# Gated cross-attention with routed experts: next rows quantised earlier, routing moved forward, two more summing steps on GpSimd in three groups of four

## The reference

```
x = x + tanh(g_xattn) * attention(layernorm(x), context)
x = x + tanh(g_ffn)   * ffn(layernorm(x))

attention: q = qdq(x) @ qdq(wq).T + bq;  k, v = split(context @ wkv.T + bkv)
           16 heads of 32;  o = softmax(q k / sqrt(32)) v;  out = qdq(o) @ qdq(wp).T + bp
           qdq rounds each row to 8-bit integers by its largest absolute value
ffn:       32 experts in 4 groups, 4 chosen per token through the best 2 groups by sigmoid(x @ gate_w.T) + bias
           each expert takes its first 128 tokens:  silu(x w1) * (x w3) @ w2, weighted, summed
           plus a shared part:  silu(x @ shared_gate) * (x @ shared_up) @ shared_down
```

## Time and profile before

| what | us |
|---|---|
| median of three runs | 3088.6 |
| lowest and highest run | 3077.08, 3096.61 |
| the profiled execution, its time | 3097.04 |
| its span in the trace | 3095.3 |

### The profile page before, as it was taken

How to read it: one execution, slowest core, us unless ns; L and a number is a source line. 1 busy time by engine, 2 the same in 40 slices (tenths; PEclk the granted TensorE clock), 3 DMA queues, 4 the chain that set the end, 5 groups by cost and what they waited for, 6 DMA issues and landing times.

```text
span 3095.3 us, 42827 instructions
## 1 busy us (share of the span) xinstructions
PE 2759.0 (89%) x14612; PEld 1140.5 (37%) x14652; DVE 1918.4 (62%) x3814; ACT 1369.7 (44%) x2436; POOL 1809.2 (58%) x1558
## 2 busy tenths in 40 slices
PE   5898999899989988989899899989999889997987
PEld 3333333333333333333333333333332334443766
DVE  6577667766776677667767766776676334343222
ACT  4155545654564466455545654564455410110111
POOL 0186667666666685667576757665677432424455
PEclk9799999999999999999999999999999999999999
DMA  3111012101211031103111311220112123232995
GB/s 127 36 51 52 24 35 73 54 22 35 76 52 40 18 91 47 44 13 98 37 35 25 97 27 36 62 65 22 35 49 63 69 89 123 72 112 70 299 292 114
DMA packets 146584, 215.56 MB, mean 70 GB/s; under 512 B 24984, under 2 KB 78232, under 8 KB 146368
## 3 DMA queue, kind: packets, MB, share of 16 engines
q1 hardware_dynamic: 130496, 195.95, 20.9%
q0 software_dynamic: 15872, 16.87, 3.0%
HBM read 126.49 MB, written 34.24 MB: 52 GB/s over the span
## 4 chain that ended last, share of the span: by engine, by line
PE 64%; DVE 14%; ACT 7%; DMA 6%; issue 6%; SPq 2%; POOL 1%; another core or an unknown queue 1%; POOLq 0%; ACTq 0%; DVEq 0%
PE o_ps L873 11%; PE s_ps L859 10%; PE r_all L748 9%; PE r_all L777 8%; PE r_all L787 8%; DVE piece_max L1312 7%; PE r_all L828 6%; DMA out_rows<-probs,slot_init 4%; ACT probs L1096 4%; PE sum_ps L886 3%; PE r_all L846 3%; SPq L555 1%; DVE amax L1166 1%; PE sum_ps L894 1%; POOL prob_acc L1581 1%
## 5 line engine op out<-in xcount | busy, mean ns | idle before, releaser
L1581 POOL TENSOR_TENSOR prob_acc<-prob_acc,probs 128x512 f32<-128x512 f32 x1140 | 1431.9, 1291 | 380.8 <-ACT probs L1096 379.2
L1096 ACT ACTIVATE probs<-s_ps 128x512 f32<-128x512 f32 (+1 forms) x1664 | 936.9, 596 | 762.6 <-PE s_ps L859 736.2
L1312 DVE TENSOR_REDUCE piece_max<-r_all 128x1 f32<-128x400 f32 (+1 forms) x2048 | 1024.9, 565 | 128.2 <-PE r_all L787 123.6
L787 PE MATMUL r_all<-k_flat,q_stack 96*128 96x400 f16 (+1 forms) x2048 | 608.5, 351 | 100.2 <-DVE piece_max L1312 55.1
L859 PE MATMUL s_ps<-q_stack,k_flat 97*128 97x512 f16 (+1 forms) x1664 | 625.8, 395 | 57.4 <-ACT probs L1096 50.6
L873 PE MATMUL o_ps<-probs,v_sb 128*32 128x512 f32 (+1 forms) x3328 | 462.5, 629 | 21.4 <-ACT probs L1096 21.4
L859 PEld LDWEIGHTS s_ps<-q_stack,k_flat 97*128 97x128 f16 (+1 forms) x1664 | 158.1, 100 | 616.0 <-ACT probs L1096 430.0
L1578 POOL COPY prob_acc<-probs 128x512 f32<-128x512 f32 x128 | 73.1, 615 | 501.9 <-PE sum_ps L894 367.1
L787 PEld LDWEIGHTS r_all<-k_flat,q_stack 96*128 96x128 f16 x2048 | 203.1, 100 | 394.5 <-DVE piece_max L1312 202.8
L1613 POOL DMA_INDIRECT slot_rows<-payload,slot x128 | 125.3, 979 | 281.9 <-DVE slot L1490 215.8
L828 PE MATMUL r_all<-probs,k_flat 128*128 128x512 f32 x512 | 223.4, 594 | 2.0 <-DVE sum_sb L1452 1.2
(11 more groups left out here) (220 smaller groups left out, 2714.4 us busy)
## 6 DMA issues: line engine op xcount, KB each, us to landing
k_flat<-k_hi SPq DMA_DIRECT2D x256, 100.1 KB, 2.2
ctx_raw<-in_ctx SPq DMA_DIRECT2D x96, 256.0 KB, 2.9
xin<-in_x SPq DMA_DIRECT2D x16, 1024.0 KB, 5.6
k_flat<-k_lo SPq DMA_DIRECT2D x128, 100.1 KB, 2.2
v_sb<-in_L_ffn_w SPq DMA_DIRECT2D x18, 512.0 KB
q_stack<-q_hi SPq DMA_DIRECT2D x256, 32.0 KB, 1.8
h_rows<-work SPq DMA_DIRECT2D x8, 1024.0 KB, 4.5
x_rows<-xin SPq DMA_DIRECT2D x8, 1024.0 KB, 6.9
```

The source lines that it names most:

```text
L787: last = nc.tensor.matmul(ps[:, 0:w], q_stack[0:KSPLIT, g % 2, j, qt * P:(qt + 1) * P], k_stack[0:KSPLIT, g % 2, j, at:at + w], start=True ...
L1096: nc.scalar.activation(probs[0:w, slot, j, :], s_ps[j % SBANKS][0:w, :], ACT.Exp).then_inc(probs_ready, 1)
L1312: V.reduce_max(piece_max[:, j * TT + qt, i:i + 1], ps[:, 0:PIECE[i]], X_AXIS).then_inc(free_of(*key), 1)
L1581: last = G.tensor_tensor(prob_acc[:, j, :], prob_acc[:, j, :], probs[:, slot, j, :], ALU.add)
```

## The change

- GpSimd adds twelve steps (0 to 11) in the groups 0, 2 and 3 of each batch, TensorE sums only step 12 there. Group 1, and the very last group, stay as they were. That is 46 steps of four adds more on GpSimd and 46 sums fewer on TensorE.
- The parts of the next rows start at step 7 of group 1 (statistics) and go on one a step: square root 8, reciprocal and shift 9, normalising 10 and 11, largest value 12; then in group 2 rounding 0 and 1, clipping 1 and 2, integers 3 and 4.
- `rows_out` writes x1 first, as soon as the statistics for the second norm are made, and `h` after it.
- For the last batch, the transposes `hT` and the logits move into the gate tiles of the batch before, into a buffer of their own; its routing runs between that batch's `add_shared`; its counts come after its first pair of gate tiles, its expert weights and slots after its first `swiglu`. The counts of the batch before come after its own third pair and those logits.
- The slot table is read back on GpSimd's queue.
- Twelve homes: two more sets of expert weights are loaded when the last `up` tile is made, into the places of the shared gate and up weights and of `ctx_lo`, one when the last `down` tile is made, and these stand on SP ahead of the output of the last batch; two more after `out_written`, in the places of the values, as before.

```diff
-PE_SUMS, LAST_PE_SUMS = (4, 8, KT - 1), (2, 4, 6, 8, 10, KT - 1)
+PE_SUMS, LONG_PE_SUMS, LAST_PE_SUMS = (4, 8, KT - 1), (KT - 1,), (2, 4, 6, 8, 10, KT - 1)
...
-FIRST_X, NEXT_X = 1, 1
+FIRST_X, NEXT_X = 1, 6
...
-HOMES, EARLY_HOMES, FREE_HOMES = 9, 7, 5
+HOMES, EARLY_HOMES, FREE_HOMES, GATE_HOMES, DOWN_HOMES = 12, 7, 5, 2, 1
...
-    return PE_SUMS if n + 1 < B * GROUPS else LAST_PE_SUMS
+    if n + 1 == B * GROUPS:
+        return LAST_PE_SUMS
+    return PE_SUMS if n % GROUPS == 1 else LONG_PE_SUMS
...
+def next_x(g, kt):
+
+    return (g - 1) * KT + kt - NEXT_X
...
-    order = gates[0:6] + [("cum", f), ("total", f)] + gates[6:]
+    counts = [("cum", f), ("total", f)]
+    down = [("down", f, t) for t in range(TT)]
+    if f == B - 1:
+        return gates[0:2] + counts + gates[2:] + down
+    if f == B - 2:
+        return (gates[0:2] + [("hT", f + 1, c) for c in range(DC)] + gates[2:3] + [("logitsT", f + 1)] + gates[3:6]
+                + [("logits", f + 1)] + counts + gates[6:] + down)
+    order = gates[0:6] + counts + gates[6:]
...
+def logits_after(f):
+
+    if f == B - 2:
+        return {("logitsT", f + 1): [0], ("up", f, 1): [1], ("gate", f, 2): [2, 3]}
+    return {("logitsT", f + 1): [0], ("down", f, 1): [1], ("down", f, 2): [2, 3]} if f + 1 < B else {}
...
-        hT, actT = probs[:, 0], probs[:, 1]
+        last_hT = ctx_lo_flat[:, 0:2 * DC * N].bitcast(FP32).rearrange("p (c n) -> p c n", c=DC)
+        hT, actT = [probs[:, 0]] * (B - 1) + [last_hT], probs[:, 1]
...
-        homes = free_blocks + late_blocks + v_blocks
+        gate_blocks = blocks_of(k_flat, range(4)) + blocks_of(ctx_lo_flat, range(2))
+        down_blocks = [probs[:, 2, 2 * i:2 * i + 2, :].rearrange("p j n -> p (j n)") for i in range(2)] + blocks_of(k_flat, [4])
...
+        homes = free_blocks + late_blocks + gate_blocks + down_blocks + v_blocks
...
             def rows_out(b):
 
+                sp.wait_ge(h_var_ready, b + 1)
+                sp.dma_start(x1_v[b], xin[:, :, :]).then_inc(x1_out, DMA)
                 sp.wait_ge(h_ready, (b + 1) * TT)
                 sp.dma_start(h_v[b], work[:, :, :]).then_inc(h_out, DMA)
-                sp.dma_start(x1_v[b], xin[:, :, :]).then_inc(x1_out, DMA)
...
                 if f == B - 1:
-                    sp.wait_ge(slots_written, B * TT * TOPK * DMA)
-                    sp.dma_start(e_slots[:, :, :], slot_v).then_inc(e_slots_in, DMA)
+                    key = ("up", f, FSC - 1)
+                    sp.wait_ge(bank_full[ring.last_bank(*key)], ring.done(*key))
+                    for e in range(EARLY_HOMES, EARLY_HOMES + GATE_HOMES):
+                        expert_weights_in(e)
+                    key = ("down", f, TT - 1)
+                    sp.wait_ge(bank_full[ring.last_bank(*key)], ring.done(*key))
+                    expert_weights_in(EARLY_HOMES + GATE_HOMES)
                 sp.wait_ge(out_ready, f + 1)
                 sp.dma_start(out_v[f], x1_in[f % 2]).then_inc(out_written, DMA)
             sp.wait_ge(out_written, B * DMA)
             sp.wait_ge(route_ready, B)
-            for e in range(EARLY_HOMES, HOMES):
+            for e in range(EARLY_HOMES + GATE_HOMES + DOWN_HOMES, HOMES):
                 expert_weights_in(e)
...
-                if g == 2 and b + 1 < B:
-                    x_part(b + 1, kt - NEXT_X)
+                if g in (1, 2) and b + 1 < B:
+                    x_part(b + 1, next_x(g, kt))
...
-                    if f and c < 2:
-                        routing[c](f)
-                    if f and c == 1:
-                        expert_masks(f)
-                    if f and c == 2:
+                    if 0 < f < B - 1:
+                        if c < 2:
+                            routing[c](f)
+                        if c == 1:
+                            expert_masks(f)
+                        if c == 2:
+                            expert_weights(f)
+                    swiglu(f, c)
+                    if f < B - 1 and c == 2:
+                        slots_of_experts(f)
+                    if f == B - 1 and c == 0:
                         expert_weights(f)
-                    swiglu(f, c)
-                    if c == 2:
                         slots_of_experts(f)
...
                 for t in range(TT):
+                    if f == B - 2 and t < 3:
+                        routing[t](f + 1)
                     add_shared(f, t)
...
+            G.dma_start(e_slots[:, :, :], slot_v).then_inc(e_slots_in, DMA)
             pool.wait_ge(h_out, B * DMA)
```

More of the change, by code:

```diff
@@ L171, in ffn_tiles @@
     gates = gate_tiles(f)
[L172 removed]
+    counts = [("cum", f), ("total", f)]
[6 more added lines that the diff above has]
+    order = gates[0:6] + counts + gates[6:]
     if f == 0:
         order += [("oiT", B - 1, c) for c in range(DC)] + [("y", B - 1, t) for t in range(TT)]
[L175 to L179 removed]
+    order += [("hT", f + 1, c) for c in range(DC)] + down[0:1] + [("logitsT", f + 1)]
+    return order + down[1:] + [("logits", f + 1)]
+def logits_after(f):
+    if f == B - 2:
+        return {("logitsT", f + 1): [0], ("up", f, 1): [1], ("gate", f, 2): [2, 3]}
+    return {("logitsT", f + 1): [0], ("down", f, 1): [1], ("down", f, 2): [2, 3]} if f + 1 < B else {}
 def steps():
@@ L928, in _ @@
                         logits_ps = open_tile(*key)
-                        logits_chunk(logits_ps, f + 1, 0)
-                        continue
-                    tile(key)
-                    if f + 1 < B and key[0] == "down" and key[2] == 1:
-                        logits_chunk(logits_ps, f + 1, 1)
-                    if f + 1 < B and key[0] == "down" and key[2] == 2:
-                        logits_chunk(logits_ps, f + 1, 2)
-                        close(logits_chunk(logits_ps, f + 1, 3), "logitsT", f + 1)
+                    else:
+                        tile(key)
+                    for c in logits_after(f).get(key, []):
+                        last = logits_chunk(logits_ps, f + 1, c)
+                        if c == DC - 1:
+                            close(last, "logitsT", f + 1)
             def rows_transposed(e):
@@ L1068, in tile @@
                     ps = full(act, *key)
-                    nc.scalar.copy(hT[:, key[2], :], ps[:, :]).then_inc(free_of(*key), 1)
+                    nc.scalar.copy(hT[b][:, key[2], :], ps[:, :]).then_inc(free_of(*key), 1)
                 elif kind == "logitsT":
@@ L1120, in _ @@
                     exp_of(s, j)
[L1121 removed]
+                    if j == 1 and g in (1, 2) and b + 1 < B and next_x(g, kt) == X_STD:
                         deviations(x_var_ready, b + 2, x_std_ready)
```

11 lines of the change are left out of this document (3 added, 8 removed).

## The result

| | us |
|---|---|
| kernel before, median of 20 runs beside those of the changed kernel | 3090.41 |
| changed kernel, median of 20 runs | 3104.28 |
| ratio, with its 95% interval | 1.0043 (1.0033 to 1.0054) |
| span of the profiled execution, before and after | 3095.3, 3104.5 |

The forecast was 54.5 us less, the change took some 14 us more (3104.28 against 3090.41). It is slower by 0.4%, well outside the range on record. The mean granted clock of the profiled execution is 0.946.

What follows compares the result with a forecast made beforehand. TensorE was taken to bound groups 2 and 3, with GpSimd having slack. Terms 14 + 11.3 - 5.5 - 47 + 68 + 10.3 + 3.4 gave 54.5 us less: 3034 us from the 3088.6 median, range 3006 to 3066.

Steps and rivals of the forecast that it cites:

- Group 0: Two sums off TensorE, 16 us less in 8 batches; minus 1.2 (first group) and 3.5 (clips): 11.3 us gained.
- the uncovered price of 12.6 us: Group 0, 7 batches: cost of the slower clips if TensorE's value tile hid none of it; 3.5 us was booked.
- GpSimd as the bound: Rival: an add takes 1.5 us instead of 1.27, group work outgrows its slack, 92 us lost, 3126 us; chance 0.04.
- Group 3: Two sums per group leave TensorE, about 2.0 us each in 7 batches: 14 us less.
- the first group: Very first group, as short as GpSimd's work: 1.2 of its 2.0 us gain taken off, 0.8 us less.
- the last batch: Its group 2: GpSimd's 58 us of work doesn't fit the 54.0 us before the next sum; 5.5 us lost.
- Group 1: Receives the next rows' statistics and following parts: 44 us plus 3 us for their load, 47 us lost.
- rival about the load: Group 1: load 4 us late in 6 batches, 3058 us, chance 0.12; or statistics hidden, 3010 us, chance 0.10.
- the dead heat: Group 1: load of x lands about 1117.7 as step 7's maxima end; 0.5 us in 6 batches, 3 us lost.
- Group 2: Next rows moved out, eight steps at 4.25 us instead of 43.96 us in all: net 9.7 us a batch, 68 us gained.
- the first rival: Group 2 stays disturbed by the context's tiles and loads and gains only its two sums: 3088 us; chance 0.14.
- The tail: From last copy to end: forward routing 10.3 us, TensorE's gap 12.38 to 2; three more homes 3.4 us; 13.7 us less.

Runs made afterwards that it cites:

- e4: Changed kernel with GpSimd's bias add after the adds of step 7 of group 0 instead of step 4: ratio 1.0041 to the kernel before.
- e3: Changed kernel with the clips of x and head outputs accessing each tile as two interleaved halves, every second element: ratio 1.0036 to the kernel before.
- e5: Changed kernel with GpSimd's bias add ahead of step 0 of group 0, its load of x issued one group earlier: ratio 0.9869 to the kernel before.
- e10: Kernel of e5 with nine homes and TensorE's sums of steps 4 and 8 back in the last batch's group 2: ratio 0.9852 to the kernel before.
- e6: Changed kernel with forward routing and extra homes undone, slot table still read back on GpSimd's queue: ratio 1.0059 to the kernel before.
- e8: Changed kernel with nine homes of expert weights instead of twelve, forward routing kept: ratio 1.0032 to the kernel before.
- e9: Changed kernel without the four clips of the head outputs at steps 5 and 6 of group 0: ratio 0.9848 to the kernel before.

## Why the prediction was wrong

**Group 0, the step that failed.** The prediction said of the clips in group 0: "+1.8 us of VectorE work, in a step in which TensorE's value tile sets the pace and hides most of it: I book 0.5". It measured 4.8 to 6.5 us of added wait for the first clip alone, of which TensorE saw 4.54 at once and the slower clock on top. So both halves failed, the price of the clip and the cover. The price came from the earlier trace rows, 2.55 us for two clips beside adds; at step 6 of group 0 the same row was 2.02. In both places the clips get in between two adds of a run of eight, and the adds there had been ready for 1.0 to 2.0 us, so GpSimd was behind ScalarE there too, by one or two adds. No row of before shows a clip behind the bias add and late in a long run, because GpSimd rested at step 4. I had asked whether GpSimd's work fits the group (58 of 85 us, it does) and how long an add takes, and not what the missing rest does to the order of its work. In fact I had written that the bias add "now comes on top of a step", and did not follow it: 4.96 us of backlog against a surplus of 0.7 us a value step lasts several steps, clips included. Even the uncovered price of 12.6 us was too small by more than a factor of three: groups 0 missed by 41 us. The Trainium skill ("SBUF — State Buffer", section "SBUF: two separate sides") says that the port pair is an exclusive lock held for the whole instruction. The waits agree that it is exclusive; in the changed kernel and in e4 they last longer than the one instruction of 1.27 us, to the end of the run of adds. That it is these ports is inferred from which operations waited and which did not; e3, meant to test it, didn't change the form. Why a clip is passed over late in such a run and not early stays open.

**GpSimd as the bound, the rival on the other side.** The right engine for the wrong reason: it had adds at 1.5 us and a group's work over its length. The 1324 adds keep GpSimd busy for 1656.4 us in all, 1.25 each (a record lasts 1.29 on average, and they overlap a little), and the group's work fits; e5 shows it with all of it in place. The kernel got slower through the order of GpSimd's work.

**Group 3, the first group, the last batch.** As worked out: -14 for -14, -1.3 for -0.8, +4.5 for +5.5. The last one was a loss seen ahead, and e10 takes it back (162.9 us, 163.4 before).

**Group 1.** +51 for +47. Neither rival about the load came: the dead heat was one, the load of x was issued 35.0 us into the group and VectorE waited 0.81 us for it, not 4; and the statistics are felt, with 2.80 us of TensorE idle behind them. Timeline of VectorE, then of TensorE, in the changed kernel:

```profile
1124.78 2.47 DVE L1245 BATCH_NORM_STATS2 stats<-xin 128x6 f32<-128x512 f32 x4 [0.81 <-DMA xin<-in_x]
```

```profile
1128.18 0.34 PE L815 MATMUL r_all<-k_flat,q_stack 96*128 96x400 f16 x1 [2.80 <-DVE piece_max L1338]
```

**Group 2.** -57 for -68. The steps without the next rows run at 4.25, as the prediction said. The slow stretch at its start stays, as the first rival had it in part. TensorE's head matmuls there, to be read beside the earlier trace rows:

```profile
1173.79 1.06 PE L901 MATMUL o_ps<-probs,v_sb 128*32 128x512 f32 x8
...
1179.83 1.12 PE L766 MATMUL r_all<-ident,ctx_raw 128*128 128x128 f32 x4 [1.44 <-DMA ctx_raw<-in_ctx]
1183.06 1.94 PE L901 MATMUL o_ps<-probs,v_sb 128*32 128x512 f32 x8
...
1188.94 1.07 PE L901 MATMUL o_ps<-probs,v_sb 128*32 128x512 f32 x8
1193.19 1.07 PE L901 MATMUL o_ps<-probs,v_sb 128*32 128x512 f32 x8
```

One step takes 9.27 us and the next 5.88, through a wait for the context's load and the clock after it (granted 0.50 from 1179.8 to 1185.0). I had put the eight steps of the earlier trace rows down to the next rows alone and let them all run at 4.25: the term was right in kind and 1.6 us a batch too large.

**The tail.** -5 for -13.7. That e6 and e8 differ by 10.2 us, where 10.3 were booked for the routing, is partly luck: e6 has a read-back of the table that the kernel before didn't have, and the shared part's tiles cost 4.0 us that were booked at 0. The homes' 3.4 are in part in the experts' pace (1.8 to 4.3 us), but I asked only what their weights delay on SP's queue, and not what they cross on the way: the landing of the scatter, 2.5 us later, and of the gathered rows, 3 us later. In the traces of before and after the gap went from 12.38 to 8.00 us, not to 2.

## What to carry to other kernels

Before work is given to an engine with slack, ask not only whether it fits but at which steps the engine will be behind its supplier, and for how long. Being an add or two behind cost a clip here one add; deep in a long run without gaps behind a lump of work it cost the rest of the run. So put lumps of work (here the bias add) where the engine waits anyway, or give it a wait where the other must get in. Weights loaded ahead are not free because the queue is idle: price what small transfers, which the next stage waits for, they will cross.

## What the hardware did that I had not expected

- A VectorE clip of 0.42 us took 5.3 to 7.0 us late in an unbroken run of GpSimd adds of 1.27 us each, and an addition of 0.69 us took 5.15. Early in such a run (8 or fewer of its instructions done) the same clip took 0.4 to 1.6 us, though GpSimd didn't pause before or after it.
- VectorE's maxima and value tiles, which read the accumulators, took their usual 0.69 us for a value tile inside a run of 20 adds (e9).
- The clip on every second element took 0.42 us, as on contiguous rows.
- With expert weights under way a small scatter landed 4.31 us after its last issue (e3), without them 1.77 (e8).
